# Gathered rows of a mixture of experts: transposed by 64 small transfers and VectorE in place of TensorE

## The chip, the cores and the metric

The kernel runs on one core of a Trainium2 chip. The metric is the device time of one execution in microseconds (us). TensorE (PE in the profile) does the matmuls, VectorE is DVE, ScalarE is ACT, GpSimd is POOL and SyncE is SP, which here only issues transfers; its queue is SPq.

## What is computed

For x of 8192 rows of 512 values, xn is the layer norm of x. The output is x + attention(xn) + experts(xn). Attention has 16 heads and windows of 64 rows. The part of the experts, with n = 8192 rows, e = 8 experts and a capacity of 1024 rows for each, is:

```python
scores = (x_flat @ Wg.T).T
top_vals, token_idx = jax.lax.top_k(scores, capacity)
token_w = jax.nn.softmax(top_vals, axis=-1)
xg = x_flat[token_idx]
h = silu(einsum('eic,ehc->eih', xg, W1)) * einsum('eic,ehc->eih', xg, W3)
y = einsum('eih,ech->eic', h, W2) * token_w[..., None]
out = zeros_like(x_flat).at[token_idx.reshape(-1)].add(y.reshape(-1, c))
```

Here c = 512 and h = 1024. Each product of float32 numbers is made of three matmuls on a high part and a low part of each operand (split3, lines 57 to 59).

## The kernel before

The program has two blocks. The attention block goes through 16 chunks of 512 rows, writes xn and the attention's output to HBM and finds the lists of rows for the experts. The expert block follows behind a barrier of all engines, and goes through 8 experts of 2 halves each. A half, numbered q = 0 to 15, has T = 512 gathered rows in TT = 4 tiles of 128.

The work of a half on each engine, in program order:

- GpSimd gathers the 512 rows with 4 indirect transfers (gather, line 168) into x_in, 128 rows on 128 partitions in each of 4 tiles, and later adds the finished rows y to the output with 4 indirect transfers (scatter, line 1568). x_in has one buffer: the gather for half q waits until the rows of half q - 1 have been read.
- TensorE turns the rows into columns: xgt (line 1664) does 16 transposes of 128x128 against the identity, from x_in into PSUM banks 0 to 3. It does this for half q + 1 between up(q) and down(q). ScalarE copies the result as the high part xgt_hi (line 1609), VectorE subtracts for the low part xgt_lo (line 1734).
- up(q) has 8 steps, m = 0 to 7, of 24 matmuls each (W1 and W3). ScalarE takes silu (line 1617), VectorE multiplies (hm, line 1754), ScalarE copies the high part of h (line 1624) and VectorE makes the low part (line 1740). hm has two buffers: step m waits for hm of step m - 2. In the first half of an expert, TensorE also does 8 small matmuls in each step (compact, line 139) that build the next expert's list, from one-hot rows of VectorE (slots_one_hot, line 127): the rows for step m + 1 are made during step m.
- down(q) has 96 matmuls with W2, and ScalarE scales the result by the weights (line 1636).

Weights come in 12 units of 512 KB for each expert: units 0 to 7 are W1 and W3, units 8 to 11 are W2. SyncE loads them into two raw buffers (load_unit, line 1544), and a load waits until the unit before the last has been split. ScalarE and VectorE split a unit in a step m (lines 1604 and 1729), right after the high and the low part of h: units 0 to 7 of expert e + 1 in steps 0 to 7 of expert e's second half, units 8 to 11 in steps 0 to 3 of its own first half. Expert 0 is different: its units 4 to 11 are split in steps 0 to 7 of half 0. Every engine does its instructions in order, so one that waits holds up all behind it; SyncE's queue has only these loads in the expert block.

Of the kernel before, what the change touches and what calls it, by code (L numbers as in the profile page):

```python
# [26 lines left out]
P = 128  # L27
N = 8192
C = 512
# [13 lines left out]
NS = CAP // P  # L43
GATE_COLS = 32
HG = 8
GROUPS = NT // HG
FAR = 11
LEAD = 6
# [6 lines left out]
def split3(nc, out, w_hi, w_lo, x_hi, x_lo, start, stop):  # L55

    nc.tensor.matmul(out, w_hi, x_hi, start=start, stop=False)  # L57
    nc.tensor.matmul(out, w_hi, x_lo, start=False, stop=False)  # L58
    return nc.tensor.matmul(out, w_lo, x_hi, start=False, stop=stop)  # L59


class Lists:
# [3 lines left out]
    def __init__(self, nc, ctx):  # L66
        def sb(name, shape, dt=F32):
            return ctx.enter_context(nc.sbuf_tensor(name, shape, dt))

        def sem(name):  # L70
            return ctx.enter_context(nc.semaphore(name))

        self.slot_a, self.slot_b = sb("slot_a", [P, E, NT], BF16), sb("slot_b", [P, E, NT], BF16)
        self.wgt, self.wgt_parts = sb("wgt", [P, E, NT]), sb("wgt_parts", [P, E, NT, 3], BF16)
        self.ident = sb("ident", [P, P])
        self.iota_b, self.iota_a = sb("iota_b", [P, P], BF16), sb("iota_a", [P, NS], BF16)
        self.iota_p, self.iota_t = sb("iota_p", [P, 1]), sb("iota_t", [P, NT], BF16)
        self.hot_a, self.hot_v = sb("hot_a", [P, NT, NS], BF16), sb("hot_v", [P, NT, 5, NS], BF16)
        self.got, self.idx_f = sb("got", [P, 5, NS]), sb("idx_f", [P, NS])
        self.idx = [sb(f"idx_{i}", [P, NS], U32) for i in range(2)]  # L80
        self.weight = [sb(f"weight_{i}", [P, NS]) for i in range(2)]

        sb("align", [P, 32])
        self.x_in, self.x_res, self.xn = (sb(n, [P, TT, C]) for n in ("x_in", "x_res", "xn"))
        self.hot_b = self.xn[:, 0:2, :].bitcast(BF16).rearrange("p a (t b) -> p a t b", b=P)

        self.raw = [self.xn[:, 2:4, :].rearrange("p a b -> p (a b)"), sb("raw", [P, 1024])[:, :]]
        self.list_step = sem("list_step")
        self.values_ready, self.hot_ready, self.hot_mm, self.got_ready, self.idx_ready = (sem(n) for n in (
            "values_ready", "hot_ready", "hot_mm", "got_ready", "idx_ready"))  # L90
        self.w_in = [sem(f"w_in_{i}") for i in range(2)]
        self.xg_in, self.out_stored = sem("xg_in"), sem("out_stored")


STEPS = 4
# [74 lines left out]
            in_offset=bass.IndirectOffsetOnAxis(ap=k.idx[par][:, tile0 + t:tile0 + t + 1], axis=0)).then_inc(k.xg_in, 16)  # L170


def attention_block(nc, d, lists):


    ctx = ExitStack()
    with ctx:
# [22 lines left out]
        ot_hi, ot_lo = sb("ot_hi", [P, G, T], F32R), sb("ot_lo", [P, G, T], F32R)  # L200
        g_sb = sb("g_sb", [P, T])

        x_f, xt_f, g_f = sb("x_f", [P, TT, C]), sb("xt_f", [P, KC, T]), sb("g_f", [P, T])
        gate_s, (above, ties, upto, exps) = x_f[:, 0, :], (xt_f[:, k, :] for k in range(KC))
        pos = ties
        hits = x_f[:, 1:3, :].rearrange("p a b -> p (a b)").bitcast(BF16)[:, 0:3 * T].rearrange("p (a b) -> p a b", a=3)
# [90 lines left out]
        def _(sp):  # L297
# [102 lines left out]
                sp.dma_start(lists.raw[u], d["w13"][0, u]).then_inc(lists.w_in[u], 16)  # L400
            store_out(NCH - 2)
            load_res(NCH - 1)
            store_out(NCH - 1)


# [1085 lines left out]
def expert_block(nc, d, lists):  # L1491

    ctx = ExitStack()
    with ctx:
# [9 lines left out]
        w2_hi, w2_lo = sb("w2_hi", [P, FM, C], F32R), sb("w2_lo", [P, FM, C], F32R)  # L1504

        h_hi, h_lo = sb("h_hi", [P, FM, T], F32R), sb("h_lo", [P, FM, T], F32R)
        xg, y, ident = lists.x_in, lists.x_res, lists.ident
        weight, raw, w_in = lists.weight, lists.raw, lists.w_in
        xgt_hi, xgt_lo = sb("xgt_hi", [P, KC, T], F32R), sb("xgt_lo", [P, KC, T], F32R)
        silu, hm = sb("silu", [P, 2, T]), sb("hm", [P, 2, T])  # L1510
        ps = ctx.enter_context(nc.psum_tensor("ps_e", [P, 8, 512], F32))
        DOWN, LISTS = 4, 7

        w_hi_ready, w_ready = sem("w_hi_ready"), sem("w_ready")
        xgt_mm, xgt_hi_ready, xgt_ready = sem("xgt_mm"), sem("xgt_hi_ready"), sem("xgt_ready")
        up1_mm, up3_mm, silu_ready, hm_ready = sem("up1_mm"), sem("up3_mm"), sem("silu_ready"), sem("hm_ready")
        h_hi_ready, h_ready = sem("h_hi_ready"), sem("h_ready")
        down_mm, y_mm, y_ready, scattered = sem("down_mm"), sem("y_mm"), sem("y_ready"), sem("scattered")
# [18 lines left out]
        @block.sync  # L1537
        def _(sp):
            def load_unit(e, u):
                n = UNITS * e + u  # L1540
                if not isinstance(n, int) or n >= 2:
                    sp.wait_ge(w_ready, n - 1)
                src = d["w13"][e, u] if u < FM else d["w2"][e, u - FM]
                sp.dma_start(raw[u % 2], src).then_inc(w_in[u % 2], 16)

            for u in range(2, UNITS):
                load_unit(0, u)
            with sp.Fori(1, E) as e:
                for u in range(UNITS):
                    load_unit(e, u)  # L1550


        @block.gpsimd
        def _(pool):
            def gather_half(q, par, tile0, e_idx):

                pool.wait_ge(lists.idx_ready, e_idx)
                pool.wait_ge(xgt_mm, KC * q)
                gather(nc, pool, lists, d["xn"], par, tile0)

            def scatter(q, par, tile0):

                for t in range(TT):
                    pool.wait_ge(y_ready, TT * q + t + 1)
                    if t == 0 and (not isinstance(q, int) or q >= 1):
                        pool.wait_ge(scattered, 16 * TT * q)
                    pool.nop(nofuse=True)  # L1567
                    nc.gpsimd.indirect_dma_start(  # L1568
                        out=d["out"], out_offset=bass.IndirectOffsetOnAxis(ap=lists.idx[par][:, tile0 + t:tile0 + t + 1], axis=0),
                        in_=y[:, t, :], in_offset=None, compute_op=ALU.add).then_inc(scattered, 16)  # L1570

            pool.wait_ge(lists.out_stored, 16 * NCH)

            def expert(e, par, first=False, last=False):
                q = HALVES * e
                gather_half(q + 1, par, TT, e + 1)
                if not first:
                    scatter(q - 1, 1 - par, TT)
                if not last:
                    gather_half(q + 2, 1 - par, 0, e + 2)  # L1580
                scatter(q, par, 0)

            expert(0, 0, first=True)
            expert(1, 1)
            with pool.Fori(1, E // 2 - 1) as i:
                expert(2 * i, 0)
                expert(2 * i + 1, 1)
            expert(E - 2, 0)
            expert(E - 1, 1, last=True)
            scatter(HALVES * E - 1, 1, TT)  # L1590
            pool.wait_ge(scattered, 16 * TT * HALVES * E)
# [3 lines left out]
        def _(act):  # L1595
# [9 lines left out]

            def xgt_hi_part(q):
                for k in range(KC):
                    act.wait_ge(xgt_mm, KC * q + k + 1)
                    nc.scalar.activation(xgt_hi[:, k, :], ps[:, k, :], ACT.Copy).then_inc(xgt_hi_ready, 1)

            def half(e, q, hf, par, splits, last=False):
                for m in range(FM):
# [42 lines left out]

        @block.tensor
        def _(pe):
            def xgt(q):
                pe.wait_ge(lists.xg_in, 16 * TT * (q + 1))
                for k in range(KC):  # L1660
                    if k % 2 == 0 and (not isinstance(q, int) or q >= 1):
                        pe.wait_ge(hm_ready, FM * q - 1 + k // 2)
                    for t in range(TT):
                        i = nc.tensor.transpose(ps[:, k, P * t:P * (t + 1)], xg[:, t, P * k:P * (k + 1)], ident[:, :])  # L1664
                    i.then_inc(xgt_mm, 1)

            def up(q, e, first_half, next_list=False):
                pe.wait_ge(xgt_ready, KC * (q + 1))
                for m in range(FM):
# [33 lines left out]
            def expert(e, last=False):  # L1703
                q = HALVES * e
                up(q, e, True, next_list=not last)
                xgt(q + 1)
                down(q, e, True, next_list=not last)
                up(q + 1, e, False)
                if not last:
                    xgt(q + 2)  # L1710

                down(q + 1, e, False, tiles=((0, 1), (2, 3)) if last else (range(TT),))

            xgt(0)
            expert(0)
            with pe.Fori(1, E - 1) as e:
                expert(e)
# [4 lines left out]
        def _(dve):  # L1722
            v = nc.vector

            def split_lo(e, u):
# [2 lines left out]
                hi, lo = unit_views(u)  # L1728
                v.tensor_tensor(lo, raw[u % 2], hi.bitcast(F32), ALU.subtract).then_inc(w_ready, 1)  # L1729

            def xgt_lo_part(q):
                for k in range(KC):
                    dve.wait_ge(xgt_hi_ready, KC * q + k + 1)
                    v.tensor_tensor(xgt_lo[:, k, :], ps[:, k, :], xgt_hi[:, k, :].bitcast(F32), ALU.subtract).then_inc(xgt_ready, 1)  # L1734

            def half(q, splits, lists_of=None, first=False):
                def lo(m):
                    n = FM * q + m
                    dve.wait_ge(h_hi_ready, n + 1)
# [2 lines left out]
                for m in range(FM):  # L1742
# [12 lines left out]
                    lo(m)  # L1755
                    if m < len(splits):
                        split_lo(*splits[m])

            def expert(e, par, first=False, last=False, second_next=True):
                q = HALVES * e  # L1760
# [5 lines left out]
                if second_next:  # L1766
                    places_one_hot(nc, dve, lists, e + 2)
                    weights_one_hot(nc, dve, lists, e + 2)
                half(q + 1, [] if last else [(e + 1, i) for i in range(FM)])
                if not last:  # L1770
                    xgt_lo_part(q + 2)

            split_lo(0, 0)
            xgt_lo_part(0)
            for u in range(1, AHEAD):
# [67 lines left out]
```

## Time and profile before

| | us |
|---|---|
| runs of the kernel, three | 2135.58, 2139.42, 2139.76 |
| median | 2139.42 |
| the profiled execution, whole time | 2137.95 |
| its span in the profile | 2136.2 |
| start of the expert block in the span | 1026.6 |
| TensorE busy | 2081.8 |

The span is what the hardware profiler saw from the first to the last instruction; 1.75 us of the profiled execution lie around it. Times of rows count from the span's start. TensorE's busy time is a sum of modelled durations of pipelined matmuls. What a matmul costs is read from the distance of one start to the next.

### The profile page before, as it was taken

The numbers are of one execution on the slowest core, as the hardware profiler recorded it, in microseconds if no ns is written. First come the engines' busy times: TensorE is split into PE (matmuls) and PEld (weight loads), VectorE is DVE, ScalarE is ACT, GpSimd is POOL, SyncE is SP. The second block draws the span as 40 slices with busy tenths as digits, with TensorE's granted clock in tenths as the row PEclk, the third lists the DMA queues.
The fourth block names the chain that finished last, engine by engine and source line by source line (L and its number), as shares of the span: only waits on it lengthen the run. The fifth ranks groups of instructions, "written<-read, shape, count | busy, mean of one in ns | idle before, by whom it ended". The sixth has DMA issues, their size and how long they took to land.

```text
span 2136.2 us, 37482 instructions
## 1 busy us (share of the span) xinstructions
PE 2081.8 (97%) x15707; PEld 1684.0 (79%) x15707; DVE 1105.8 (52%) x1664; ACT 670.1 (31%) x1035; POOL 518.4 (24%) x308
## 2 busy tenths in 40 slices
PE   7999999999999999988899999999999999999997
PEld 5877777777777888866688888888888888888886
DVE  6665666666667777667643534344333443334211
ACT  3333323223334343332333232233232322324221
POOL 2333333333332333344011112111121111201111
PEclk9999999999999999999899999999999999999999
DMA  6211223233232101111333233232331423314211
GB/s 207 77 59 62 80 80 106 80 98 122 82 102 81 44 37 41 60 61 60 126 91 86 73 79 89 52 95 59 88 89 45 112 59 70 97 49 100 58 20 20
DMA packets 68485, 165.44 MB, mean 77 GB/s; under 512 B 5648, under 2 KB 6032, under 8 KB 68368
## 3 DMA queue, kind: packets, MB, share of 16 engines
q1 hardware_dynamic: 54032, 130.24, 18.8%
q0 software_dynamic: 14336, 33.56, 8.8%
q8 instruction: 83, 1.36, 0.3%
q14 instruction: 34, 0.28, 0.0%
HBM read 112.40 MB, written 51.38 MB: 77 GB/s over the span
## 4 chain that ended last, share of the span: by engine, by line
PE 51%; DVE 0%; POOL 0%; ACT 0%; issue 0%; POOLq 0%
PE ps_e L57 17%; PE ps_e L58 16%; PE ps_e L59 16%; PE ps_e L1664 1%; PE ps_e L139 1%; POOL out_rows L1568 0%; DVE xgt_lo L1734 0%; ACT x_res L1636 0%; DVE w_lo L1729 0%; ACT w_hi L1604 0%; POOLq L1567 0%
## 5 line engine op out<-in xcount | busy, mean ns | idle before, releaser
L57 PE MATMUL ps_e<-xgt_hi,w_hi 128*128 128x512 f32 x1024 | 404.3, 395 | 2.8 <-DVE xgt_lo L1734 2.8
L59 PE MATMUL ps_e<-xgt_hi,w_lo 128*128 128x512 f32 x1024 | 399.1, 390 | 0.0
L58 PE MATMUL ps_e<-xgt_lo,w_hi 128*128 128x512 f32 x1024 | 398.9, 390 | 0.0
L1754 DVE TENSOR_TENSOR hm<-ps_e,silu 128x512 f32<-128x512 f32 x128 | 88.5, 692 | 531.9 <-PE ps_e L59 531.2
L57 PEld LDWEIGHTS ps_e<-xgt_hi,w_hi 128*128 128x128 f32 x1024 | 192.6, 188 | 41.0 <-DVE xgt_lo L1734 3.0
L59 PEld LDWEIGHTS ps_e<-xgt_hi,w_lo 128*128 128x128 f32 x1024 | 192.5, 188 | 40.7
L168 POOL DMA_INDIRECT x_in<-xn_rows,idx x64 | 75.9, 1186 | 612.1 <-DVE idx L160 303.8
L58 PEld LDWEIGHTS ps_e<-xgt_lo,w_hi 128*128 128x128 f32 x1024 | 192.8, 188 | 37.9
L449 POOL TENSOR_TENSOR pn_sb<-p_sb,s_rec 128x1024 f32<-128x1024 f32 x64 | 122.3, 1911 | 390.0 <-DVE s_rec L1120 389.9
L57 PE MATMUL ps<-xt_hi,wqk_hi 128*128 128x512 f32 x512 | 211.3, 413 | 0.0
L1624 ACT ACTIVATE h_hi<-hm 128x512 fp32r<-128x512 f32 x128 | 81.0, 632 | 392.3 <-DVE hm L1754 389.4
L57 PE MATMUL ps_e<-w_hi,h_hi 128*128 128x512 f32 x512 | 200.7, 392 | 0.0
L59 PE MATMUL ps<-xt_hi,wqk_lo 128*128 128x512 f32 x512 | 200.2, 391 | 0.0
L58 PE MATMUL ps<-xt_lo,wqk_hi 128*128 128x512 f32 x512 | 200.0, 391 | 0.0
L58 PE MATMUL ps_e<-w_lo,h_hi 128*128 128x512 f32 x512 | 199.4, 390 | 0.0
L59 PE MATMUL ps_e<-w_hi,h_lo 128*128 128x512 f32 x512 | 199.2, 389 | 0.0
L1568 POOL DMA_INDIRECT out_rows<-x_res,idx x64 | 100.7, 1573 | 332.9 <-ACT x_res L1636 318.4
L441 POOL TENSOR_TENSOR s_sb<-s_sb,s_max 128x1024 f32<-128x1024 f32 x64 | 124.2, 1940 | 211.5 <-DVE s_max L1112 211.5
L509 ACT ACTIVATE q_sb<-ps,q_bias 128x512 f32<-128x512 f32 x64 | 44.1, 689 | 411.0 <-PE ps L59 410.9
L1740 DVE TENSOR_TENSOR h_lo<-hm,h_hi 128x512 fp32r<-128x512 f32 x128 | 88.7, 693 | 94.2 <-ACT h_hi L1624 93.4
L1636 ACT ACTIVATE x_res<-ps_e,weight 128x512 f32<-128x512 f32 x64 | 43.0, 690 | 286.1 <-PE ps_e L59 286.1
L1160 DVE COPY pt_diag<-ps 64x512 f32<-64x512 f32 x128 | 88.9, 694 | 82.3 <-PE ps L801 77.5
(176 smaller groups left out, 3602.6 us busy)
## 6 DMA issues: line engine op xcount, KB each, us to landing
xn<-in_w SPq DMA_DIRECT2D x48, 512.0 KB, 3.6
raw<-in_w SPq DMA_DIRECT2D x48, 512.0 KB
x_res<-in_x SPq DMA_DIRECT2D x16, 1024.0 KB, 5.6
out_rows<-x_res SPq DMA_DIRECT2D x16, 1024.0 KB, 4.2
xn_rows<-xn SPq DMA_DIRECT2D x11, 1024.0 KB, 5.1
x_in<-in_x SPq DMA_DIRECT2D x10, 1024.0 KB, 7.7
x_f<-in_x SPq DMA_DIRECT2D x5, 1024.0 KB, 5.3
xn_rows<-x_f SPq DMA_DIRECT2D x5, 1024.0 KB, 10.1
```

The costliest lines, as they stand in the source:

```text
L57: nc.tensor.matmul(out, w_hi, x_hi, start=start, stop=False)
L58: nc.tensor.matmul(out, w_hi, x_lo, start=False, stop=False)
L59: return nc.tensor.matmul(out, w_lo, x_hi, start=False, stop=stop)
L168: nc.gpsimd.indirect_dma_start(out=k.x_in[:, t, :], out_offset=None, in_=xn_rows, in_offset=bass.IndirectOffsetOnAxis(ap=k.idx[par][:, til ...
L441: nc.gpsimd.tensor_tensor(s_sb[:, :, :, :], s_sb[:, :, :, :], s_max[:, :].rearrange("p (t h) -> p t h", t=TT).unsqueeze(3) .to_broadcast([ ...
L449: nc.gpsimd.tensor_tensor(pn_sb[:, :, :, :], p_sb[:, :, :, :], s_rec[:, :].rearrange("p (t h) -> p t h", t=TT).unsqueeze(3) .to_broadcast( ...
L509: nc.scalar.activation(q_sb[:, :], ps[:, QB, :], ACT.Identity, bias=q_bias[:, g:g + 1], scale=SCALE).then_inc(q_ready, 1)
L1160: i = nc.vector.tensor_copy(out, src)
L1568: nc.gpsimd.indirect_dma_start(out=d["out"], out_offset=bass.IndirectOffsetOnAxis(ap=lists.idx[par][:, tile0 + t:tile0 + t + 1], axis=0), ...
L1624: nc.scalar.activation(h_hi[:, m, :], hm[:, m % 2, :], ACT.Copy).then_inc(h_hi_ready, 1)
L1740: v.tensor_tensor(h_lo[:, m, :], hm[:, m % 2, :], h_hi[:, m, :].bitcast(F32), ALU.subtract).then_inc(h_ready, 1)
L1754: v.tensor_tensor(hm[:, m % 2, :], ps[:, 2 * (m % 2) + 1, :], silu[:, m % 2, :], ALU.mult).then_inc(hm_ready, 1)
```

## The change

The 16 transposes of TensorE for a half go. In their place SyncE issues 64 transfers from SBUF to SBUF (spread): for each of the 4 tiles, each group a of 32 partitions (a quadrant) and each group i of 32 columns, the 32x32 blocks (a, i) of the four column groups k go to the 32 partitions of quadrant i. One transfer moves 32 partitions x 4 pieces of 128 bytes, 16 KB. The target is xs, a new tile that attention had as xt_f. VectorE then transposes all 32x32 blocks of xs in place with 4 instructions of 128x512 (turn_blocks), and the high and low parts are read from xs and not from PSUM.

The order of the work changes too:

- spread for half 0 stands in the attention block's SyncE queue, ahead of the last store of the output.
- spread for half 1 stands in SyncE's queue ahead of the load of unit 7 of expert 0.
- For an expert e of 1 or more, spread for its first half (2e) stands ahead of the load of unit 4, and that for its second half (2e + 1) behind the load of unit 11. Spread waits for the gathered rows and for xgt_lo of the half before.
- turn_blocks(q + 1) stands in steps 4 to 7 of half q on VectorE, one instruction in each; the first waits for all 64 transfers. For half 0 all four stand ahead of VectorE's first split of the expert block.
- The gather waits for the spread of the half before (xs_in) and not for the transposes.
- SyncE's loop over the experts is written out.

```diff
+def spread(nc, sp, k):
+    rows = k.xs[:, :, :].rearrange("p a b -> p (a b)").rearrange("p (b k c) -> p b k c", k=KC, c=QD)
+    for t in range(TT):
+        for a in range(NQ):
+            for i in range(NQ):
+                sp.dma_start(rows[QD * i:QD * (i + 1), NQ * t + a, :, :],
+                             by_tile(k.x_in[QD * a:QD * (a + 1), t, :])[:, :, i, :]).then_inc(k.xs_in, 16)
+
+SPREAD = 16 * TT * NQ * NQ
...
             load_res(NCH - 1)
+            sp.wait_ge(lists.xg_in, 16 * TT)
+            sp.wait_ge(wgt_copied, 1)
+            spread(nc, sp, lists)
             store_out(NCH - 1)
...
-            for u in range(2, UNITS):
-                load_unit(0, u)
-            with sp.Fori(1, E) as e:
-                for u in range(UNITS):
+            def spread_half(q):
+                sp.wait_ge(lists.xg_in, 16 * TT * (q + 1))
+                sp.wait_ge(xgt_ready, KC * q)
+                spread(nc, sp, lists)
+
+            def expert(e, last=False):
+                for u in range(2, UNITS):
+                    if u == FM // 2 and e >= 1:
+                        spread_half(HALVES * e)
+                    if u == FM - 1 and e == 0:
+                        spread_half(1)
                     load_unit(e, u)
+                if e >= 1:
+                    spread_half(HALVES * e + 1)
+                if not last:
+                    load_unit(e + 1, 0)
+                    load_unit(e + 1, 1)
...
-                pool.wait_ge(xgt_mm, KC * q)
+                pool.wait_ge(lists.xs_in, SPREAD * q)
...
-                    act.wait_ge(xgt_mm, KC * q + k + 1)
-                    nc.scalar.activation(xgt_hi[:, k, :], ps[:, k, :], ACT.Copy).then_inc(xgt_hi_ready, 1)
+                    act.wait_ge(xgt_turned, KC * q + k + 1)
+                    nc.scalar.activation(xgt_hi[:, k, :].rearrange("p (b c) -> p b c", c=QD), xs[:, :, k, :], ACT.Copy).then_inc(xgt_hi_ready, 1)
...
                 up(q, e, True, next_list=not last)
-                xgt(q + 1)
                 down(q, e, True, next_list=not last)
                 up(q + 1, e, False)
-                if not last:
-                    xgt(q + 2)
...
+            def turn_blocks(q, k):
+
+                if k == 0:
+                    dve.wait_ge(lists.xs_in, SPREAD * (q + 1))
+                v.transpose(xs[:, :, k, :], xs[:, :, k, :]).then_inc(xgt_turned, 1)
...
                     if m < len(splits):
                         split_lo(*splits[m])
+                    if not last and m >= FM // 2:
+                        turn_blocks(q + 1, m - FM // 2)
...
+            for k in range(KC):
+                turn_blocks(0, k)
             split_lo(0, 0)
             xgt_lo_part(0)
```

## Rows read from the trace of the kernel before

**Rows 1.** The page's first part: busy us of TensorE, share, instructions.

```profile
PE 2081.8 (97%) x15707; PEld 1684.0 (79%) x15707; DVE 1105.8 (52%) x1664; ACT 670.1 (31%) x1035; POOL 518.4 (24%) x308
```

**Rows 2.** The chain in order of time: start us, us, work; first and last transposes.

```profile
1079.15 1.95 PE ps_e L1664 x16
...
2036.36 1.95 PE ps_e L1664 x16
```

**Rows 3.** Timeline, SyncE: start us, us issuing; last store and expert block's loads.

```profile
1025.80 0.38 SPq L327 DMA_DIRECT2D out_rows<-x_res  x1
...
1044.09 0.33 SPq L1544 DMA_DIRECT2D xn<-in_w  x1
...
1117.59 0.33 SPq L1544 DMA_DIRECT2D raw<-in_w  x1
...
1185.49 0.33 SPq L1544 DMA_DIRECT2D raw<-in_w  x1
```

**Rows 4.** Timeline, SyncE: transfers issued back to back.

```profile
5.24 0.71 SPq L306 DMA_DIRECT2D same<-in_same  x1
...
568.66 1.31 SPq L319 DMA_DIRECT2D gate_rows<-g_sb  x4
...
636.49 1.46 SPq L361 DMA_DIRECT2D xt_f<-gate_rows  x3
```

**Rows 5.** Transfers of 4 small stores and 4 more, 568 to 575 us.

```profile
DMA packets 128, 0.13 MB, mean 19 GB/s; under 512 B 64, under 2 KB 64, under 8 KB 128
...
q1 hardware_dynamic: 128, 0.13, 9.3%
```

**Rows 6.** Transfers with rows of 2 KB, 615 to 628 us.

```profile
q1 hardware_dynamic: 1056, 2.10, 51.7%
```

**Rows 7.** Issue to landing: the loads of line 1544, then those of line 361.

```profile
DMA to landing us min/median/max: 3.2/3.6/5.2
...
DMA to landing us min/median/max: 2.7/3.3/4.9
```

**Rows 8.** Timeline, TensorE and its weight loads (PEld), expert block.

```profile
1031.38 0.80 PE L57 MATMUL ps_e<-xgt_hi,w_hi 128*128 128x512 f32 x1 [2.81 <-DVE xgt_lo L1734]
...
1035.59 0.37 PE L139 MATMUL ps_e<-hot_v,xn 128*128 128x40 bf16 x8
...
1102.49 0.19 PEld L57 LDWEIGHTS ps_e<-xgt_hi,w_hi 128*128 128x128 f32 x1
...
1178.44 0.37 PE L139 MATMUL ps_e<-hot_v,xn 128*128 128x40 bf16 x8
...
1207.26 0.37 PE L139 MATMUL ps_e<-hot_v,xn 128*128 128x40 bf16 x8
```

**Rows 9.** Timeline, ScalarE, steps 4 and 5 of half 1.

```profile
1131.45 1.04 ACT L1604 ACTIVATE w_hi<-xn 128x1024 fp32r<-128x1024 f32 x1
...
1136.89 1.04 ACT L1604 ACTIVATE w_hi<-raw 128x1024 fp32r<-128x1024 f32 x1
```

**Rows 10.** Timeline, VectorE: block's start, then step 4 of half 2.

```profile
1027.70 1.23 DVE L1729 TENSOR_TENSOR w_lo<-xn,w_hi 128x1024 fp32r<-128x1024 f32 x1 [1.94 <-ACT w_hi L1604]
...
1200.42 0.69 DVE L1740 TENSOR_TENSOR h_lo<-hm,h_hi 128x512 fp32r<-128x512 f32 x1 [0.70 <-ACT h_hi L1624]
1201.03 1.22 DVE L127 TENSOR_TENSOR xn<-slot_b,iota_b 128x1024 bf16<-128x1024 bf16 x1
```

**Rows 11.** Groups by line, from 1024 us on: busy us, mean ns.

```profile
L1734 DVE TENSOR_TENSOR xgt_lo<-ps_e,xgt_hi 128x512 fp32r<-128x512 f32 x64 | 39.6, 681 | 0.0
```

**Rows 12.** Timeline, GpSimd: the last gather of half 0.

```profile
993.47 0.95 POOL L168 DMA_INDIRECT x_in<-xn_rows,idx  x1 [0.30 <-issue]
```

**Rows 13.** Windows: length, busy us (count) of each engine, TensorE's granted clock, DMA.

```profile
1028.60:1031.30 2.70, 0.00 (x0) 0.00 (x0) 2.70 (x6) 1.96 (x4) 0.47 (x1) 0.92 0.69 195
1031.40:1034.30 2.90, 2.90 (x7) 2.33 (x8) 1.70 (x2) 1.06 (x1) 2.29 (x3) 0.51 0.72 205
1034.40:1036.00 1.60, 1.60 (x15) 1.17 (x14) 0.48 (x1) 0.00 (x0) 1.09 (x2) 1.00 0.92 315
```

More of the change, by code:

```diff
@@ L45 @@
 HG = 8
+QD = 32
+NQ = P // QD
 GROUPS = NT // HG
@@ L59, in split3, with by_tile @@
     return nc.tensor.matmul(out, w_lo, x_hi, start=False, stop=stop)
+def by_tile(row):
+    return row.rearrange("p (k i c) -> p k i c", i=NQ, k=KC)
 class Lists:
@@ L84, in __init__ @@
         self.x_in, self.x_res, self.xn = (sb(n, [P, TT, C]) for n in ("x_in", "x_res", "xn"))
+        self.xs = sb("xs", [P, KC, T])
         self.hot_b = self.xn[:, 0:2, :].bitcast(BF16).rearrange("p a (t b) -> p a t b", b=P)
@@ L91, in __init__ @@
         self.w_in = [sem(f"w_in_{i}") for i in range(2)]
-        self.xg_in, self.out_stored = sem("xg_in"), sem("out_stored")
+        self.xg_in, self.out_stored, self.xs_in = sem("xg_in"), sem("out_stored"), sem("xs_in")
 STEPS = 4
@@ L201, in attention_block @@
         g_sb = sb("g_sb", [P, T])
-        x_f, xt_f, g_f = sb("x_f", [P, TT, C]), sb("xt_f", [P, KC, T]), sb("g_f", [P, T])
+        x_f, xt_f, g_f = sb("x_f", [P, TT, C]), lists.xs, sb("g_f", [P, T])
         gate_s, (above, ties, upto, exps) = x_f[:, 0, :], (xt_f[:, k, :] for k in range(KC))
@@ L1506, in expert_block @@
         h_hi, h_lo = sb("h_hi", [P, FM, T], F32R), sb("h_lo", [P, FM, T], F32R)
-        xg, y, ident = lists.x_in, lists.x_res, lists.ident
+        y = lists.x_res
         weight, raw, w_in = lists.weight, lists.raw, lists.w_in
+        xs = lists.xs[:, :, :].rearrange("p a b -> p (a b)").rearrange("p (b k c) -> p b k c", k=KC, c=QD)
         xgt_hi, xgt_lo = sb("xgt_hi", [P, KC, T], F32R), sb("xgt_lo", [P, KC, T], F32R)
@@ L1514, in expert_block @@
         w_hi_ready, w_ready = sem("w_hi_ready"), sem("w_ready")
-        xgt_mm, xgt_hi_ready, xgt_ready = sem("xgt_mm"), sem("xgt_hi_ready"), sem("xgt_ready")
+        xgt_turned, xgt_hi_ready, xgt_ready = sem("xgt_turned"), sem("xgt_hi_ready"), sem("xgt_ready")
         up1_mm, up3_mm, silu_ready, hm_ready = sem("up1_mm"), sem("up3_mm"), sem("silu_ready"), sem("hm_ready")
@@ L1544, in load_unit @@
                 sp.dma_start(raw[u % 2], src).then_inc(w_in[u % 2], 16)
-            for u in range(2, UNITS):
-                load_unit(0, u)
-            with sp.Fori(1, E) as e:
-                for u in range(UNITS):
-                    load_unit(e, u)
+            def spread_half(q):
[8 more added lines that the diff above has]
+                        spread_half(1)
+                    load_unit(e, u)
+                if e >= 1:
[3 more added lines that the diff above has]
+                    load_unit(e + 1, 1)
+            for e in range(E):
+                expert(e, last=e == E - 1)
         @block.gpsimd
@@ L1657, in _ @@
         def _(pe):
[L1658 to L1665, printed above, removed]
             def up(q, e, first_half, next_list=False):
@@ L1705, in expert @@
                 up(q, e, True, next_list=not last)
-                xgt(q + 1)
                 down(q, e, True, next_list=not last)
                 up(q + 1, e, False)
-                if not last:
-                    xgt(q + 2)
                 down(q + 1, e, False, tiles=((0, 1), (2, 3)) if last else (range(TT),))
-            xgt(0)
             expert(0)
@@ L1733, in xgt_lo_part, with half @@
                     dve.wait_ge(xgt_hi_ready, KC * q + k + 1)
-                    v.tensor_tensor(xgt_lo[:, k, :], ps[:, k, :], xgt_hi[:, k, :].bitcast(F32), ALU.subtract).then_inc(xgt_ready, 1)
-            def half(q, splits, lists_of=None, first=False):
+                    v.tensor_tensor(xgt_lo[:, k, :].rearrange("p (b c) -> p b c", c=QD), xs[:, :, k, :],
+                                    xgt_hi[:, k, :].bitcast(F32).rearrange("p (b c) -> p b c", c=QD), ALU.subtract).then_inc(xgt_ready, 1)
+            def half(q, splits, lists_of=None, first=False, last=False):
                 def lo(m):
@@ L1768, in expert @@
                     weights_one_hot(nc, dve, lists, e + 2)
-                half(q + 1, [] if last else [(e + 1, i) for i in range(FM)])
+                half(q + 1, [] if last else [(e + 1, i) for i in range(FM)], last=last)
                 if not last:
                     xgt_lo_part(q + 2)
+            for k in range(KC):
+                turn_blocks(0, k)
             split_lo(0, 0)
```

## The prediction

> **What bounds the kernel now.** I read the page's first part first: TensorE is busy for 2081.8 of 2136.2 us [rows 1], so nothing else is likely to be the bound. The chain that ended last says what TensorE does there: in the expert block its 16 transposes stand in the chain, 1.95 us for each half from half 1 to half 15, one after the other [rows 2]. The transposes are on the path, and taking them out can give time back. Then I asked what the change puts elsewhere, so I read SyncE's queue [rows 3, 4], the times to landing [rows 7], and the order of VectorE, ScalarE and TensorE around steps 4 to 6 of a half [rows 8 to 10]. The reader is to see two periods there: a step of up takes 5.76 us in a first half (1178.44 to 1207.26 is five steps [rows 8]) and 5.44 us in a second half (ScalarE's splits at 1131.45 and 1136.89 [rows 9]). TensorE does not wait in them, so each wait that outlasts its slack is lost time.
>
> **What goes.** 15 groups of transposes inside the stream, 15 x 1.95 = 29.3 us. The group of half 0 lies in the start of the block and is counted there.
>
> **What VectorE gains in work.** Four transposes of 128x512 for each half. No row shows one. The nearest is a subtraction of the same shape at 0.68 us [rows 11]; below, I can think of none that makes it free, above, the 128x1024 operation takes 1.22 us [rows 10]. I take 0.68, as the shape is the same. In step 4 of a first half VectorE has nothing to do between 1202.3 and 1204.8, since slots_one_hot ends at 1201.03 + 1.22 and the next hm waits for TensorE, so 0.68 and even 1.22 us lie in idle time: priced at nothing. If that cover were gone it would cost at most 4 x 1.22 us for each half. High and low parts from SBUF in place of PSUM: same shapes, priced at nothing; they stand before down(q) ends, some 20 us before they are needed.
>
> **The price of a spread, S.** S is the time from the issue of the first to the issue of the last of 64 transfers. What a spread's transfer costs SyncE no row shows; these are the bounds. Four stores of 8 partitions each take 1.31 us, 0.33 each [rows 4]: S = 21.1. Three transfers of 128 pieces each back to back take 1.46 us, 0.49 each: S = 31.2. When the queue is deep, at the program's start, one took 0.71 us, and I let 0.725 with its distance to the next stand for that: S = 46.4. The engines that move the data give another bound. One spread transfer has 128 pieces over 16 engines, 8 each, plus one packet of completion. Between 615 and 628 us, 1056 packets took 51.7% of 16 x 13 us, 102 ns each, nearly all of 2 KB [rows 6]. Between 568 and 575 us, 128 packets took 9.3% of 16 x 7 us = 10.4 us; half are of 2 KB and half are under 512 bytes [rows 5]. With 95 to 102 ns for the large ones, 57 to 68 ns are left for a small one; I use 60. Then a transfer takes 9 x 60 ns = 0.54 us of each engine, S = 34.6; if a small piece cost as much as a large one, 9 x 95 ns = 0.855 us, S = 54.7. I take 31.2, since these transfers too have 128 pieces each and the small packets' 34.6 lies close; S = 21.1 and 54.7 stay for the range.
>
> [...] No row of this trace is a transfer within SBUF.
>
> **Where S meets the path.** Three places, each with what stands behind it.
>
> Second halves (1, 3, ... 13; seven). SyncE issues unit 3 at 1117.59 [rows 3], and then the spread for the next half from 1118.0. The load of unit 4 stands behind all 64. It went at 1123.03 before, and now goes at 1118.0 + S and lands 3.6 us later [rows 7]. ScalarE splits unit 4 in step 4, at 1131.45 before [rows 9], and silu, hm and the high part of step 5 are queued behind that split. TensorE's step 7 needs hm of step 5. Half 1's up begins at 1102.49 [rows 8], so step 7 begins at 1102.49 + 7 x 5.44 = 1140.6; before it come 1.04 for the split, 0.60 for silu, 0.69 for hm and some 0.2 between them. The load must land by 1138.1. Loss: 1118.0 + S + 3.6 - 1138.1 = S - 16.5.
>
> First halves (2, 4, ... 14; seven). The spread begins behind unit 11, at 1185.49 + 0.4 = 1185.9 [rows 3], and lands 2.7 us after its last issue, the shortest of line 361 [rows 7]. VectorE comes to turn_blocks at 1201.1, after the low part of step 4 [rows 10], and waits there. Behind it in its queue is slots_one_hot (1.22 us) for TensorE's compact of step 6, at 1207.26 [rows 8]. VectorE must be free of the wait by 1207.26 - 1.22 - 0.68 = 1205.4. Loss: 1185.9 + S + 2.7 - 1205.4 = S - 16.8.
>
> Half 0. The spread begins behind unit 6, 1044.09 + 0.4 = 1044.5 [rows 3]. The load of unit 7 is behind it and lands at 1044.5 + S + 3.6. Its split is in step 3, and VectorE's slots_one_hot for step 5 is queued behind it. Step 5's compact stands at 1035.59 + 5 x 5.76 = 1064.4 [rows 8]; less 1.22, 1.23, 1.04 and 0.1, the load must land by 1060.8. Loss: S - 12.7.
>
> The start. The first gather's last issue ends at 994.4 [rows 12], its rows are in by some 997.5 (with the 2.7 to 3.6 us of other transfers [rows 7], an estimate). The spread ends its issue at 997.5 + S and lands 2.7 us later. VectorE then does 4 x 0.68, a split of 1.23 and four low parts of some 0.62 from start to start, 6.4 us, before TensorE can begin; it began at 1031.38 [rows 8]. With a spread in time the block's start costs 1026.7 + 6.4 - 1031.4 = 1.7; otherwise 997.5 + S + 2.7 + 6.4 - 1031.4 = S - 24.8, from S = 26.5 on. The last store, at 1025.8 before [rows 3], is held up by less than that.
>
> The clock. [...] 15 waits of over 10 us at 1.5 each: 22.5. Waits of 4 us may cost it or not, 0 to 22.5.
>
> **Sum.** From S = 26.5: -29.3 + (S - 24.8) + 7 (S - 16.5) + 7 (S - 16.8) + (S - 12.7) + 22.5 = 16 S - 277.4. With 31.2 that is +221.8, on the profiled execution's own 2137.95 (0.07% below the median of the runs): 2359.8, about 2360 us. The shares: transposes -29, start +6, second halves +103, first halves +101, half 0 +18.5, clock +22.5.
>
> **Rivals.**
> Cheap transfers. SyncE issues each in 0.33 us, and the engines keep up. 15 S - 273.4 and 0 to 22.5 for the clock: +43 to +66, 2181 to 2204 us. For it: the isolated load also has 0.33 us [rows 3]. Against: those back to back with 128 pieces take more. [...]
> [...]
> Not slower. All waits stay in their slack and the 29.3 us remain. The point that decides: 15 S = 273.4, S = 18.2, or 0.285 us for each transfer. At 0.275, S = 17.6, second halves lose 1.1, first 0.8, half 0 4.9 us, the start 1.7: -9, about 2129 us. For it: the losses stand only in S. Against: the quickest back to back in the trace is 0.33 [rows 4], and 8 partitions are fewer than 32.
>
> **How the numbers follow.** My forecast, 0.43, has its own range from S = 26.9 (0.42 us) to 34.6: 2291 to 2414 us. Cheap transfers have 0.25, dear ones 0.25, not slower 0.07. For the range I leave out the 0.07 and the dearer half of the dear ones: 2180 to 2605. Within 0.2% is what a measurement of this kernel can't tell from no change. Faster 0.05, same 0.02, slower 0.93, from the same cases.
>
> **What would show it.** SyncE's row of 64 issues has S directly: 64 x 0.49. In second halves ScalarE waits for the load in step 4 (line 1604), in first halves VectorE's transpose waits for transfers some 15 us, TensorE has one gap in each half of 14 to 15 us with half clock behind it, and no line 1664. The VectorE transpose has some 0.68 us. [...]

## The result and the profile after

The changed kernel takes 2525.57 us, median of 4 runs (2525.09 to 2527.63), against 2139.31 us for the kernel before (4 runs): 1.181 times as long, 95% interval 1.179 to 1.183. Forecast were 2360 us and a range of 2180 to 2605. The profiled execution took 2526.01 us with a span of 2524.2.

First the page's first part, with the chain's shares by engine behind it. TensorE's busy time has hardly moved from [rows 1], though 256 transposes, 16 x 1.95 = 31.2 us, are gone: as the part on the clock shows, the matmuls behind each wait ran slower and took about as much more. TensorE's share fell from 97% to 83%.

```profile
PE 2083.3 (83%) x15451; PEld 1677.9 (66%) x15451; DVE 1142.2 (45%) x1728; ACT 670.5 (27%) x1035; POOL 513.9 (20%) x308
...
PE 63%; SPq 25%; DVE 4%; issue 3%; DMA 3%; ACT 2%; POOL 0%; DVEq 0%; ACTq 0%; POOLq 0%
```

SPq, the issuing of SyncE's queue, was nowhere in the chain before and is a quarter of it now. The list of waits from 1030 us on, TensorE alone, says where (who waits for whom, us in total, times, longest us):

```profile
PE ps_e L59 <- DVE hm L1788: 202.9, 8, 26.5
PE ps_e L147 <- DVE xn L135: 166.6, 7, 28.1
PE ps_e L59 <- DVE xgt_lo L1767: 21.4, 1, 21.4
```

These are 16 waits, one for the start and one for each of 15 halves, in the places that the prediction named: hm of step 5 in second halves, the one-hot rows for compact in first halves. The one exception is half 14: the last expert makes no next list, so there TensorE waits for hm, which is why hm has 8 waits and the one-hot rows 7 (half 0 and six first halves). Together they are 390.9 us. What stands behind them is to be read in two halves. This is the timeline of half 1, SyncE, then ScalarE and VectorE around step 4, then TensorE:

```profile
1160.89 0.33 SPq L1570 DMA_DIRECT2D raw<-in_w  x1
1161.32 38.91 SPq L188 DMA_DIRECT2D xs<-x_in  x60
...
1199.62 3.18 SPq L188 DMA_DIRECT2D xs<-x_in  x5
1202.84 0.59 SPq L1570 DMA_DIRECT2D xn<-in_w  x1
...
1206.63 1.06 ACT L1645 ACTIVATE w_hi<-xn 128x1024 fp32r<-128x1024 f32 x1 [31.66 <-DMA xn<-in_w]
1207.60 0.58 ACT L1658 ACTIVATE silu<-ps_e 128x512 f32<-128x512 f32 x1
...
1207.72 1.23 DVE L1756 TENSOR_TENSOR w_lo<-xn,w_hi 128x1024 fp32r<-128x1024 f32 x1 [32.02 <-ACT w_hi L1645]
1208.86 0.70 DVE L1762 STREAM_TRANSPOSE xs<-xs 128x512 f32<-128x512 f32 x1
1209.49 0.65 DVE L1788 TENSOR_TENSOR hm<-ps_e,silu 128x512 f32<-128x512 f32 x1
...
1210.20 0.80 PE L59 MATMUL ps_e<-xgt_hi,w_hi 128*128 128x512 f32 x1 [25.81 <-DVE hm L1788]
```

The 64 transfers are issued from 1161.3 to 1202.8 (the two rows are parts of an answer by windows and share one transfer at their border). Only then does the load of unit 4 go, 3.8 us later ScalarE can split it, and silu, hm and TensorE's step 7 follow one by one. The VectorE transpose that stands behind waits for nothing: the transfers have landed.

In half 2 the same engines wait in another order. First SyncE, then VectorE's first transpose of step 4 and the one-hot rows behind it, then TensorE:

```profile
1255.40 41.81 SPq L188 DMA_DIRECT2D xs<-x_in  x64
...
1298.48 0.71 DVE L1762 STREAM_TRANSPOSE xs<-xs 128x512 f32<-128x512 f32 x1 [27.76 <-DMA xs<-x_in]
1299.12 1.18 DVE L135 TENSOR_TENSOR xn<-slot_b,iota_b 128x1024 bf16<-128x1024 bf16 x1
...
1300.36 0.45 PE L147 MATMUL ps_e<-hot_v,xn 128*128 128x40 bf16 x8 [23.34 <-DVE xn L135]
```

A spread takes 41 to 43 us to issue (42.0 for half 1's), 0.65 us for each transfer, not 31. Line 188's own row, and its time to landing, beside a window of nothing but such transfers (1010 to 1030 us: packets, then the queue's packets, MB and share of the 16 engines):

```profile
L188 SPq DMA_DIRECT2D xs<-x_in x1024: 585/601/1921, 995.7 to 2415.2; - x171
...
DMA to landing us min/median/max: 1.8/1.8/3.4
```

```profile
DMA packets 4347, 0.50 MB, mean 25 GB/s; under 512 B 4346, under 2 KB 4346, under 8 KB 4346
...
q1 hardware_dynamic: 4346, 0.50, 15.8%
```

The 16 engines are busy for 15.8% of 20 us: 4346 packets in 16 x 3.16 us, 11.6 ns each: 3866 of 128 bytes and 480 of 4 bytes, one to eight, which I take for the completions. The data lands 1.8 us after its issue. So the transfers themselves are no limit; the time is SyncE's, in issuing.

### The profile page after: what moved, and what is told of

Its sections match the earlier page's. It is cut to its first block, busy times and chain, and to the rows that moved or that the text cites. A ratio compares the mean times of both kernels' runs of the same rounds, so it can differ in the third digit from the quotient of the medians.

```text
span 2524.2 us, 37795 instructions
## 1 busy us (share of the span) xinstructions
PE 2083.3 (83%) x15451; PEld 1677.9 (66%) x15451; DVE 1142.2 (45%) x1728; ACT 670.5 (27%) x1035; POOL 513.9 (20%) x308
## 4 chain that ended last, share of the span: by engine, by line
PE 63%; SPq 25%; DVE 4%; issue 3%; DMA 3%; ACT 2%; POOL 0%; DVEq 0%; ACTq 0%; POOLq 0%
SPq L188 24%; PE ps L59 9%; PE ps_e L59 9%; PE ps_e L60 9%; PE ps_e L61 9%; PE ps L60 8%; PE ps L61 8%; PE ps L839 2%; PE ps L826 2%; PE ps L775 2%; PE ps L730 1%; DMA xn<-in_w 1%; ACT w_hi L1645 1%; DVE w_lo L1756 1%; PE ps L740 1%
## 5 line engine op out<-in xcount | busy, mean ns | idle before, releaser
L59 PE MATMUL ps_e<-xgt_hi,w_hi 128*128 128x512 f32 x1024 | 418.8, 409 | 224.3 <-DVE hm L1788 202.9
L60 PE MATMUL ps_e<-xgt_lo,w_hi 128*128 128x512 f32 x1024 | 410.2, 401 | 0.0
L61 PE MATMUL ps_e<-xgt_hi,w_lo 128*128 128x512 f32 x1024 | 409.7, 400 | 0.0
L59 PEld LDWEIGHTS ps_e<-xgt_hi,w_hi 128*128 128x128 f32 x1024 | 200.4, 196 | 268.5 <-DVE hm L1788 183.8
L61 PEld LDWEIGHTS ps_e<-xgt_hi,w_lo 128*128 128x128 f32 x1024 | 199.2, 195 | 43.6
L60 PEld LDWEIGHTS ps_e<-xgt_lo,w_hi 128*128 128x128 f32 x1024 | 200.7, 196 | 40.5
L1756 DVE TENSOR_TENSOR w_lo<-xn,w_hi 128x1024 fp32r<-128x1024 f32 x48 | 58.8, 1224 | 235.3 <-ACT w_hi L1645 235.3
L147 PE MATMUL ps_e<-hot_v,xn 128*128 128x40 bf16 x448 | 21.2, 184 | 166.6 <-DVE xn L135 166.6
L1762 DVE STREAM_TRANSPOSE xs<-xs 128x512 f32<-128x512 f32 x64 | 44.8, 703 | 208.7 <-DMA xs<-x_in 208.7
```

## The experiments

The two theories of the first four runs: SyncE's price is one for each transfer, or it grows with the pieces. The rival on the product's side, that VectorE's transposes or reading from SBUF cost something, is tested by the same runs, since all the rest of the change stays in them. In the diffs below, .then_inc and some loops and helpers are left out, and a comment names the run where two or more share a block.

**e_merge16.** The diff against the changed kernel, in spread and at the two readers:

```diff
+    x_all = k.x_in[:, :, :].rearrange("p t (k i c) -> p (t k) i c", k=KC, i=NQ)
-    for t in range(TT):
+    for t in range(0, TT, 4):
         for a in range(NQ):
             for i in range(NQ):
-                sp.dma_start(rows[QD * i:QD * (i + 1), NQ * t + a, :, :],
-                             by_tile(k.x_in[QD * a:QD * (a + 1), t, :])[:, :, i, :]).then_inc(k.xs_in, 16)
+                sp.dma_start(rows[QD * i:QD * (i + 1), TT * a + t:TT * a + t + 4, :, :].rearrange("p b k c -> p (b k) c"),
+                             x_all[QD * a:QD * (a + 1), KC * t:KC * (t + 4), i, :]).then_inc(k.xs_in, 16)
-SPREAD = 16 * TT * NQ * NQ
+SPREAD = 16 * (TT // 4) * NQ * NQ
...
-  nc.scalar.activation(xgt_hi[:, k, :].rearrange("p (b c) -> p b c", c=QD), xs[:, :, k, :], ACT.Copy)
+  nc.scalar.activation(by_rows(xgt_hi[:, k, :]), xs_t[:, :, :, k, :], ACT.Copy)
```

The low part is read in the same way; xs_t is xs seen as "p (a t k c) -> p t a k c", by_rows is "p (t a c) -> p t a c".

> The changed kernel with the spread of a half as 16 transfers of 64 KB (32 partitions x 16 pieces of 128 bytes) in place of 64 of 16 KB; the block order in xs is turned (quadrant outside tile) so that one access pattern covers the four tiles. Same bytes, same pieces. Theory 1, the price is one per transfer on the SyncE queue (0.66 us each in the changed kernel): issuing takes 16 x 0.66 = 10.6 us, under the point of 18.2, all waits go, -29.3 + 1.7: about 2112 us, faster than the kernel before by 1.3%. Theory 2, the price goes with the pieces (8 per engine and transfer): issuing takes 42 us as now, and the time stays near 2525 us. Theory 3, both parts count: in between.

Measured: 2108.03 us (4 runs), 0.987 of the kernel before, measured beside it (2135.82), interval 0.985 to 0.988. It beats both kernels. In the halves TensorE has no wait of this kind any more, and its busy time is down by more than the transposes' 31.2 us. The page's first part, then SyncE's rows for one spread, with the loads around it, in half 1:

```profile
PE 2046.1 (97%) x15451; PEld 1655.6 (79%) x15451; DVE 1144.4 (54%) x1728; ACT 672.9 (32%) x1035; POOL 512.5 (24%) x308
...
1115.74 0.33 SPq L1576 DMA_DIRECT2D raw<-in_w  x1
1116.18 10.77 SPq L189 DMA_DIRECT2D xs<-x_in  x16
1126.99 0.62 SPq L1576 DMA_DIRECT2D xn<-in_w  x1
```

0.67 us for a transfer with four times the pieces, 0.03 us more than with one quarter of them. Theory 1 holds, and the gain of 27.8 us agrees with the 29.3 - 1.7 = 27.6 of the prediction's two terms that are left; the interval of the ratio allows 25 to 32 us.

**e_merge32.** The same with steps of 2 tiles: 32 transfers of 32 KB.

> The same with 32 transfers of 32 KB (32 partitions x 8 pieces). Theory 1, per transfer: issuing takes 32 x 0.66 = 21.1 us, by the prediction's sum for that S +43 to +66 us: 2182 to 2205 us, with waits of 4 to 5 us in each half. Theory 2, per piece: near 2525 us.

Measured: 2198.04 us (4 runs), 1.028 of before, interval 1.026 to 1.030. A spread takes 21.8 us to issue. TensorE's waits:

```profile
PE ps_e L59 <- DVE hm L1794: 40.6, 8, 6.8
PE ps_e L147 <- DVE xn L135: 25.5, 7, 9.1
PE ps_e L59 <- DVE xgt_lo L1773: 7.7, 1, 7.7
```

Half 14's wait is again one for hm; it was 1.8 us. So a wait was 5.5 us in second halves, (40.6 - 1.8) / 7, and 2.6 in first ones, (25.5 - 9.1 + 1.8) / 7; half 0 had 9.1. For S = 21.8 the prediction's terms are 5.3, 5.0 and 9.1: first halves lost only half as much. The total fits none the less, because the clock took more than the 0 to 22.5 us that the prediction left for such waits (about 28, worked out below).

**e_onepiece and e_whole512.** 64 transfers of one piece on each of 32 partitions, 128 or 512 bytes. The first leaves out three of the four column groups, the second the order of the columns that the product needs; both have the changed kernel's waits and queues:

```diff
-                sp.dma_start(rows[QD * i:QD * (i + 1), NQ * t + a, :, :],
-                             by_tile(k.x_in[QD * a:QD * (a + 1), t, :])[:, :, i, :])
+                sp.dma_start(rows[QD * i:QD * (i + 1), NQ * t + a, 0, :],             # e_onepiece
+                             by_tile(k.x_in[QD * a:QD * (a + 1), t, :])[:, 0, i, :])
+                sp.dma_start(rows[QD * i:QD * (i + 1), NQ * t + a, :, :].rearrange("p k c -> p (k c)"),  # e_whole512
+                             k.x_in[QD * a:QD * (a + 1), t, P * i:P * (i + 1)])
```

> The changed kernel with 64 transfers of only one piece of 128 bytes on each of 32 partitions (the other three column groups are left out, so xs holds old values there). Theory 1, per transfer: 0.66 us each remain, about 2525 us. Theory 2, per piece: a quarter of the pieces, about 0.33 us each as for the small stores, S = 21, 2182 to 2205 us.

> The changed kernel with 64 transfers of the same bytes, each of one piece of 512 bytes on 32 partitions (the columns of x_in come in another order than the product wants). Theory 1, per transfer whatever its shape: 0.66 us each, about 2525 us. Theory 2, the number of pieces or the third dimension of the pattern costs the time: about 0.33 to 0.49 us each, S = 21 to 31, 2182 to 2360 us. If it differs from the run with one piece of 128 bytes, the bytes count too.

Measured, one run each: 2507.36 and 2509.85 us; a spread takes 41.2 and 41.4 us to issue. A quarter of the pieces saves 0.8 us of 42. Neither the number of pieces nor the third dimension is what is dear.

**e_from_hbm, e_to_hbm, e_128_rows, e_8_rows.** What then makes these transfers take 0.65 us, when those that the prediction took the price from took 0.49? Each run changes the 64 transfers and nothing else; none of them brings the gathered rows to where the product wants them. The first two keep e_whole512's shape, 32 partitions x 512 bytes, so that only the memory at one end differs from it.

```diff
+                sp.dma_start(rows[QD * i:QD * (i + 1), NQ * t + a, :, :].rearrange("p k c -> p (k c)"),  # e_from_hbm
+                             k.src[r:r + QD, 0:P])                                                      # src = x, in HBM
+                sp.dma_start(k.dst[r:r + QD, :], k.x_in[QD * a:QD * (a + 1), t, P * i:P * (i + 1)])     # e_to_hbm
...
+        sp.dma_start(flat[:, QD * n:QD * (n + 1)], x_flat[:, QD * n:QD * (n + 1)])                      # e_128_rows
...
+            sp.dma_start(flat[8 * g:8 * (g + 1), C * t:C * t + P], k.x_in[8 * g:8 * (g + 1), t, 0:P])   # e_8_rows
```

Here r counts 32 rows for each transfer; flat and x_flat are xs and x_in with all that lies behind the partition as one dimension.

> The changed kernel with the 64 transfers of 32 partitions x 512 bytes read from the input x in HBM and not from SBUF (xs gets other rows than the gathered ones). Theory A, the 0.64 us for an issue belongs to transfers with SBUF on both sides: 0.33 to 0.49 us here, S = 21 to 31, the time by the prediction's sum 2182 to 2360 us. Theory B, it belongs to 32 partitions or to a long row of issues: 0.64 us again, near 2510 us.

> The changed kernel with the 64 transfers of 32 partitions x 512 bytes written from x_in to HBM and not to SBUF (xs keeps what it held). Theory A, SBUF on both sides makes an issue dear: 0.47 us as for the transfers from HBM, S = 30, by the prediction's sum 2347 us. Theory D, SBUF as the source makes it dear: 0.64 us, near 2510 us.

> The changed kernel with 64 transfers within SBUF of 128 partitions x 128 bytes, each partition to itself (no quadrant is moved, so xs is not what the product wants). Theory A, SBUF on both sides: 0.64 us again, near 2510 us. Theory B, 32 partitions are what is dear (2 for each of 16 engines): 0.33 to 0.49 us, 2182 to 2360 us.

> The changed kernel with 64 transfers within SBUF of 8 partitions x 512 bytes, a quarter of the data (xs holds old values elsewhere). The kernel before has stores of 8 partitions to HBM at 0.33 us. Theory A, SBUF on both sides: 0.64 us, near 2510 us. Theory C, the number of engines that a transfer is split over sets it (8 in place of 16): 0.33 us, S = 21, 2182 to 2205 us.

The spread for half 1, issued in half 0, in SyncE's timeline, in this order (one row for each kernel):

```profile
1049.67 30.41 SPq L189 DMA_DIRECT2D xs<-in_x  x64
```

```profile
1047.20 30.74 SPq L189 DMA_DIRECT2D scratch_rows<-x_in  x64
```

```profile
1057.73 41.49 SPq L187 DMA_DIRECT2D xs<-x_in  x64
```

```profile
1057.90 42.71 SPq L188 DMA_DIRECT2D xs<-x_in  x64
```

The kernels took 2346.33, 2343.95, 2518.19 and 2547.58 us, one run each. With HBM on one side, either one, an issue takes 0.48 us; with SBUF on both sides it takes 0.65 to 0.67, with 8, 32 or 128 partitions. A transfer of e_8_rows has 8 packets of 4 bytes in the trace where one of the changed kernel has 16, and was no cheaper. Theories B, C and D fall, A stands. It is not the whole account of an issue's price: the kernel before's four stores of 8 partitions to HBM took 0.33 us each, in a row too [rows 4], and no run here tells why they are cheaper than the 0.48.

The first run also tests the prediction's sum away from its guess of S: 16 x 30.4 - 277.4 = +209, 2347 us, where 2346.33 was measured. So close a match is in part luck. TensorE's waits in that kernel, and that of half 14:

```profile
PE ps_e L59 <- DVE hm L1789: 109.1, 8, 14.7
PE ps_e L147 <- DVE xn L135: 85.9, 7, 16.4
PE ps_e L59 <- DVE xgt_lo L1768: 10.3, 1, 10.3
...
2238.53 0.77 PE L59 MATMUL ps_e<-xgt_hi,w_hi 128*128 128x512 f32 x1 [10.26 <-DVE hm L1789]
```

Second halves lost 14.1 us each (13.9 by the sum), but first halves 11.4 (13.6 by the sum), half 0 16.4 (17.7) and the start 5.0 (5.6). What the sum has too much there, some 16 us with the second halves counted in, is about what it has too little for the clock, 22.5 where TensorE lost 37.5 us outside its waits.

**e_turn_late.** Are the losses in first and second halves separate?

```diff
-                    if not last and m >= FM // 2:
-                        turn_blocks(q + 1, m - FM // 2)
...
+                turn_all(q + 1)          # the four turn_blocks, one after the other
                 xgt_lo_part(q + 1)
...
                 if not last:
+                    turn_all(q + 2)
                     xgt_lo_part(q + 2)
```

> The changed kernel with its four VectorE transposes moved from steps 4 to 7 of a half to the end of its steps, just ahead of the low part of the gathered rows. The 64 transfers stay where they are. Theory 1, the two losses are separate, VectorE's wait in first halves and the load of unit 4 behind the transfers in second halves: in first halves the transfers land 60 us into the half, transposes and low parts end at 65, before the next up at 68, so the seven waits of about 26 us go with their clock: 2525 - 7 x 27 = 2335 us, and second halves keep their gaps. Theory 2, SyncE's queue is the bound of an expert (two spreads of 42 us and 12 loads): less is won, over 2450 us.

Measured: 2346.05 us (4 runs), 1.098 of before, interval 1.096 to 1.100. TensorE's waits:

```profile
PE ps_e L59 <- DVE hm L1792: 176.7, 7, 25.7
PE ps_e L147 <- DVE xn L135: 29.1, 1, 29.1
PE ps_e L59 <- DVE xgt_lo L1771: 22.5, 1, 22.5
```

The waits of the seven first halves are gone; those of the seven second halves (25.2 us each), of half 0 and of the start are within 1.1 us of what they were. VectorE still waits in first halves, as its row at the end of half 2 shows, but no more ahead of the one-hot rows or hm:

```profile
1301.33 2.49 DVE L1762 STREAM_TRANSPOSE xs<-xs 128x512 f32<-128x512 f32 x4 [11.26 <-DMA xs<-x_in]
```

64 transfers of 0.65 us are free where only VectorE waits for them, late; they cost 25 us where a load of weights stands behind them.

**e_merge16_late.** The same diff on top of e_merge16.

> The kernel with 16 transfers of 64 KB, with the four VectorE transposes at the end of a half's steps in place of steps 4 to 7. Theory 1: at S = 11 the transfers have landed long before, the transposes are hidden at either place, 2108 us as with 16 transfers alone, within 0.2%. Theory 2: transposes in steps 4 to 7 delay hm or the one-hot rows a little, and the time falls by some us; or they hold up the next up at the end, and it rises.

Measured: 2107.30 us (4 runs), 0.987 of before, interval 0.986 to 0.989; no difference from e_merge16 can be told. The placing of VectorE's transposes matters only while S is long.

## Why the prediction was right, and where it was off

**What bounds the kernel, and what goes.** Right. The transposes were on the path: with the waits removed, 27.8 us came back where 27.6 were expected.

**VectorE's work.** Right. A transpose of 128x512 takes 0.70 us (0.68 was taken), and it is hidden: in e_merge16 TensorE needs 1075.8 us from the first matmul of up(0), at 1030.68, to the end, where the kernel before needs 1075.6 without its transposes (2136.2 - 1031.4 - 29.3). So nothing else of the change costs time that can be told.

**The price of a spread.** This is the term that was off, in size: 42 us and not 31.2. The prediction took the price from back to back transfers between HBM and SBUF, 0.49 us [rows 4]. That is what such transfers cost here too, 0.48 us, but the spread's have SBUF on both sides, and 0.65. No row of the kernel before has one. The bound from the engines was worse: 60 ns for a small packet, worked out of [rows 5], is 11.6 ns. The trace of the kernel before, packet by packet, shows the error. The 64 small packets of those rows were completions of 4 bytes and took 9 ns each; the 64 of 2 KB took 154 ns each, and not the 95 to 102 that the prediction carried over from [rows 6]. So what it ascribed to small packets was time of the large ones. That its 34.6 us lay beside the 31.2, and S then came out at 42, not far above both, is chance: the engines, at 15.8%, set no limit here. The same 1 MB costs SyncE 42 us in 64 transfers and 11 in 16 (e_merge16).

**Where S meets the path.** Right in each of the places, and a little too dear in three of them. The terms for S = 42 beside what was measured, in us:

| | by the prediction's terms | measured |
|---|---|---|
| transposes gone | -29.3 | -29.3 (as in [rows 2]) |
| the start | 17.2 | 14.3 |
| seven second halves | 7 x 25.5 = 178.5 | 7 x 25.8 = 180.8 |
| seven first halves | 7 x 25.2 = 176.4 | 7 x 22.9 = 160.6 |
| half 0 | 29.3 | 28.1 |
| the clock | 22.5 | 33 |
| sum | 394.6 | 388 |

These are the rows that the measured ones need besides the list of waits, the start and half 14:

```profile
1045.63 0.79 PE L59 MATMUL ps_e<-xgt_hi,w_hi 128*128 128x512 f32 x1 [21.37 <-DVE xgt_lo L1767]
...
2418.54 0.76 PE L59 MATMUL ps_e<-xgt_hi,w_hi 128*128 128x512 f32 x1 [22.09 <-DVE hm L1788]
```

Second halves: (202.9 - 22.1) / 7. First halves: (166.6 - 28.1 + 22.1) / 7. The start's loss is not its wait of 21.4 us, which also covers where TensorE waited and transposed before; it is 1045.63 - 1031.38 [rows 8]. There the spread began at 995.7 and not at 997.5, and landed 1.8 us after its last issue and not 2.7. The landing is also 0.9 us of the 2.3 that a first half lost less; the spreads issued in halves 1 to 14, mostly a little over 41 us, are another half a microsecond, and the rest stays open. In second halves the landing of the spread has no part, since the load behind it is what counts.

**The clock.** Right in kind, too small in size. In half 1 the granted clock fell during the wait and was at 0.50 when it ended; the windows before, at and behind its end (length, busy us and count of each engine, granted clock, DMA):

```profile
1176.00:1209.00 33.00, 8.39 (x38) 6.60 (x36) 1.28 (x2) 1.54 (x2) 3.24 (x4) 0.67 0.27 66
1209.00:1213.00 4.00, 2.80 (x7) 2.22 (x8) 3.05 (x5) 2.06 (x3) 0.77 (x1) 0.50 0.79 278
1213.50:1219.00 5.50, 5.50 (x24) 4.45 (x23) 3.94 (x6) 2.25 (x4) 0.00 (x0) 0.90 0.51 130
```

From 1210.20 some ten matmuls ran at 0.43 us from start to start in place of 0.23, 2 us lost; behind the wait of half 2 it was six, 1.2 us. Over the 15 halves it was 5 to 13 each, 122 in all, 24 us. The whole is larger: from the first matmul of up(0) to the end TensorE needs 2524.2 - 1045.6 - (390.9 - 21.4) = 1109.1 us outside its waits, against the kernel before's 1075.6. That is the 33 us of the table, 2.2 for each wait. No run shows the prediction's 1.5 as the price of a wait: behind the one of 2.81 us in the kernel before [rows 8] the first seven matmuls took 3.04 us, from 1031.38 to the next start at 1034.42, where 7 x 0.23 are 1.61, so 1.4 us, at a granted clock of 0.51 [rows 13]. Since e_merge16 without such waits has 1075.8, all of it belongs to the waits; how the part beyond the 24 us comes about was not followed. Short waits cost it too: the same difference in e_merge32 is 28 us, for 15 waits of 1.8 to 9.1.

**The sum.** 16 x 42 - 277.4 = +394.6, 2533 us on the profiled execution's 2137.95; the changed kernel's was 2526.01, +388. With the right S the sum is 6 us too high, but that is what remains of two larger errors that offset each other, some 18 us too much over the waits and some 11 too little for the clock.

**The rivals.** The one that came nearest is that of dear transfers, the S of 46.4 to 54.7 from its bounds for a spread, 2603 to 2736 us by its sum. The 46.4 came from 0.71 us at the program's start, where the engines were busy all the time (101.8% by the sum of the packets' times, 3 to 8 us) and transfers landed some 7.3 us after their issue. Here the engines were at 15.8%, and what was dear is SyncE's own time for an issue. Cheap transfers (2181 to 2204 us) is what half as many give, 2198, with the offsetting told at e_merge32. The point that decides, S = 18.2, is borne out from both sides: 21.8 is slower than before, 11 is faster; no run lies between.

## What to carry to other kernels

Count transfers before bytes: on a queue that also carries the loads which a kernel lives on, each issue had a price of its own here, 0.48 to 0.69 us in a row of 16 to 64, and what stood behind a block of them went late by all of it. Merge them along whatever dimension can be made uniform by choosing the order of the blocks in the target, as here quadrant outside tile; that turned 18% slower into 1.3% faster. And when a wait can't be shortened, look at what is queued behind the waiting instruction: once VectorE's wait stood at the end of the steps, it cost TensorE nothing. Two other ways were not tried: to issue the loads of weights ahead of the 64 transfers, and to issue the transfers from another engine.

## What was not expected of the hardware

A transfer issued by SyncE takes 0.33 us alone (loads of weights), 0.48 us in a row of 64 with HBM at one end and 32 partitions at the other, and 0.64 to 0.69 us in a row of 16 to 64 with SBUF at both ends, with 8 to 512 pieces and 4 to 64 KB (each kernel's spread for half 1). With 8 partitions the two are furthest apart: 0.33 us for each of four stores to HBM in a row [rows 4], 0.67 within SBUF (e_8_rows). Behind such a row in the changed kernel the first load too took 0.59 us and the second 0.43 before they were at 0.33 again. Why two ends in SBUF are dearer stays open. A packet of 128 bytes within SBUF took an engine about 12 ns, a completion of 4 bytes 9 ns; a packet of 2 KB, in the small stores of [rows 5], 154 ns.
